# The last stage of a graph kernel, finished in three parts of its nodes, with the output bias on TensorE

## The chip, the cores and the metric

The kernel runs on one NeuronCore of a Trainium2 chip. The metric is the device time of one execution in microseconds; of several executions the median is taken. PE is TensorE, DVE is VectorE, ACT is ScalarE, POOL is GpSimd, SP is SyncE, which only issues DMAs here.

## What is computed

A graph of 6250 nodes with 128 features each and 200000 edges goes through a graph convolution of five rounds, a residual with a row normalisation, an attention over the edges with eight heads, and a second residual with a row normalisation. The change concerns only the end of the attention layer and what follows it:

```python
def _layernorm(x, axis=-1, eps=1e-05):
    m = jnp.mean(x, axis=axis, keepdims=True)
    v = jnp.var(x, axis=axis, keepdims=True)
    return (x - m) / jnp.sqrt(v + eps)
...
        w = es / (denom[row] + 1e-08)
        msg = w[..., None] * V[col]
        out = jax.ops.segment_sum(msg, row, num_segments=n).reshape(n, -1)
        return out @ wo + bo
...
    x = _layernorm(x + _L1_gnn_ref(x, edge_index, edge_attr_64, ...), axis=-1)
    return x
```

## The kernel before

The program is one chain of stages. Every engine runs its part of each stage in program order: adjacency, convolution, `project` (first normalisation, queries, keys and values), `attend` (attention over the edges) and `finish`. Each part is a Python function for one engine (`dve_fin`, `pe_fin`, `act_fin`, `sp_fin`), and the engines are joined by semaphores, so the order on an engine is the order in which the code stands.

Nodes lie in tiles of 128 rows: `NB` = 49 tiles, the last with 106 nodes. `BATCHES` groups them by four: batches 0 to 11 have four tiles, batch 12 has one. `x1` holds the first layer's output (in the profile it is called `deg`, whose memory it uses), `acc` the attention's sums for each node, 128 values and 8 denominators (`h` in the profile).

`finish` works batch by batch, with two PSUM banks for the transposes (`PS[:, n % 2]`) and two for the products (`PS[:, 2 + n % 2]`):

- DVE, `weigh(n)` (L2132): divides a batch's sums by their denominators into `o`, tile by tile.
- PE, in `pe_fin`: transposes the batch (L2105), and then, one batch behind, `products(n - 1)` (L2096) multiplies the previous batch by `wo`. A product in fp32 shows as two matmul records, a transpose as one.
- ACT (L2116): evacuates the transposed batch from PSUM to `ot`.
- DVE, `residual(n)`: adds the product to `x1` (L2140), adds the bias `bo` (L2142), and takes the statistics of each tile (`bn_stats`, L2144).

DVE's order is weigh 0, weigh 1, and for each n: weigh n + 2, residual n. Behind the last batch DVE aggregates the statistics of all 49 tiles (L2154), adds epsilon (L1406), lets ACT take all square roots in one instruction (L2118), takes reciprocals (L1409), and normalises the 49 tiles one by one in place (L2158). SP stores each batch of four tiles when its tiles are normalised (L2086, the last one at L2088), 256 KB each.

`L` (`Chain.link`) makes DVE wait for its own instruction before it goes on. In `project` the first layer is normalised in another way, which the change takes over: `GROUPS` cuts the nodes into three parts, `to_root(g)` aggregates a part's statistics, ACT takes its roots, `scales(g)` makes scale and bias of each node, and ACT normalises tiles with an Identity activation, with the scale and bias as pointers (L1487). `x1_ready` counts the 49 tiles of that stage, `x1_scales_ready` its three parts.

Of the kernel before, what the change touches and what calls it, by code (L numbers as in the profile page):

```python
# [5 lines left out]
FP32 = mybir.dt.float32  # L6
# [4 lines left out]
ALU = mybir.AluOpType  # L11
# [3 lines left out]
P = 128  # L15
# [92 lines left out]
class Kernel:  # L108
# [5 lines left out]
    def sem(self, name):  # L114
        if name not in self.sems:
            self.sems[name] = self.stack.enter_context(self.nc.semaphore(name))
        return self.sems[name]
# [1282 lines left out]
BATCHES = [(t, min(4, NB - t)) for t in range(0, NB, 4)]  # L1400


def normalise(k, v, ch, V, mv, rooted_sem, root_sem, x1):

    L = ch.link
    L(V.tensor_scalar(mv[:, :, 2], mv[:, :, 1], EPS, None, ALU.add))  # L1406
    V.memset(k.vecs[:, 3:4], 0.0).then_inc(root_sem, 1)
    v.wait_ge(rooted_sem, 1)
    L(V.reciprocal(mv[:, :, 2], mv[:, :, 3]))  # L1409


def project(k, stack):

    nc, sem, PS, io = k.nc, k.sem, k.ps, k.io
# [652 lines left out]
def finish(k, out):  # L2067

    nc, sem, PS, io = k.nc, k.sem, k.ps, k.io
    with ExitStack() as s:  # L2070
# [7 lines left out]
        acc = k.h[:, :].rearrange("p (t c) -> p t c", c=MW)  # L2078
        ready, turned, ot_ready, prod, taken = (sem("f_" + n) for n in ("ready", "turned", "ot_ready", "products", "taken"))
        root, rooted, normal, stored = (sem("f_" + n) for n in ("to_root", "rooted", "normal", "stored"))  # L2080
        def sp_fin(sp):
            full = len(BATCHES) - 1
            for n, (t, m) in enumerate(BATCHES):
                sp.wait_ge(normal, t + m)
                if n < full:
                    sp.dma_start(out[t * P:(t + m) * P, :].rearrange("(t p) f -> p t f", p=P), x1[:, t:t + m, :]).then_inc(stored, 16)  # L2086
                else:
                    sp.dma_start(out[t * P:N, :], x1[0:NL, t, :]).then_inc(stored, 16)  # L2088
            sp.wait_ge(stored, 16 * len(BATCHES))

        def products(pe, n):
            pe.wait_ge(ot_ready, n + 1)
            if n >= 2:
                pe.wait_ge(taken, n - 1)
            for x in range(BATCHES[n][1]):
                last = nc.tensor.matmul(PS[:, 2 + n % 2, x * P:(x + 1) * P], ot[:, n % 2, x, :], wo[:, :], start=True, stop=True)  # L2096
            last.then_inc(prod, 1)

        def pe_fin(pe):
# [9 lines left out]
            products(pe, len(BATCHES) - 1)  # L2109

        def act_fin(act):
            for n, (t, m) in enumerate(BATCHES):
                act.wait_ge(turned, n + 1)
                if n >= 2:
                    act.wait_ge(prod, n - 1)
                nc.scalar.activation(ot[:, n % 2, 0:m, :].rearrange("p j c -> p (j c)"), PS[:, n % 2, 0:m * P], ACT.Copy).then_inc(ot_ready, 1)  # L2116
            act.wait_ge(root, 1)
            nc.scalar.activation(mv[:, :, 3], mv[:, :, 2], ACT.Sqrt).then_inc(rooted, 1)  # L2118

        def dve_fin(v):  # L2120
            V = nc.vector
            ch = Chain(v, sem("dve_chain"), k.links)
            L = ch.link
            L(V.tensor_scalar(inv[:, :, :], acc[:, :, D:MW], 1e-8, None, ALU.add))
            L(V.reciprocal(inv[:, :, :].rearrange("p t h -> p (t h)"), inv[:, :, :].rearrange("p t h -> p (t h)")))

            def weigh(n):
                t, m = BATCHES[n]
                if n >= 2:
                    v.wait_ge(turned, n - 1)  # L2130
                for x in range(m):
                    last = V.tensor_tensor(o[:, n % 2, x, :].rearrange("p (h d) -> p h d", d=DK), acc[:, t + x, 0:D].rearrange("p (h d) -> p h d", d=DK),  # L2132
                                           inv[:, t + x, :].rearrange("p (h o) -> p h o", o=1).broadcast_to([P, HEADS, DK]), ALU.mult)
                last.then_inc(ready, 1)

            def residual(n):
                t, m = BATCHES[n]
                rows = x1[:, t:t + m, :]
                v.wait_ge(prod, n + 1)
                V.tensor_tensor(rows, rows, PS[:, 2 + n % 2, 0:m * P].rearrange("p (t f) -> p t f", f=D), ALU.add).then_inc(taken, 1)  # L2140
                v.wait_ge(taken, n + 1)
                L(V.tensor_tensor(rows, rows, bo[:, :].rearrange("p (o f) -> p o f", o=1).broadcast_to([P, m, D]), ALU.add))  # L2142
                for x in range(t, t + m):
                    last = V.bn_stats(st[:, x, :], x1[:, x, :])  # L2144
                return last
            weigh(0)
            weigh(1)
            for n in range(len(BATCHES)):
                if n + 2 < len(BATCHES):
                    weigh(n + 2)  # L2150
                last = residual(n)
            L(V.memset(k.vecs[:, 0:1], 0.0))
            for x in range(NB):
                last = V.bn_aggr(mv[:, x, 0:2], st[:, x, :])  # L2154
            L(last)
            normalise(k, v, ch, V, mv, rooted, root, x1)
            for x in range(NB):
                V.tensor_scalar(x1[:, x, :], x1[:, x, :], mv[:, x, 0:1], mv[:, x, 2:3], ALU.subtract, ALU.mult).then_inc(normal, 1)  # L2158

        return dve_fin, pe_fin, act_fin, sp_fin  # L2160
# [29 lines left out]
```

## Time and profile before

| | us |
|---|---|
| median of 3 runs | 4229.77 |
| the runs | 4227.85 to 4234.28 |
| the profiled execution, its own time | 4231.56 |
| its span in the profile | 4229.8 |
| `finish` within the span, from its first instruction on DVE (4165.31) | 64.5 |

| engine | busy, us | share of the span |
|---|---|---|
| PE | 3654.2 | 86% |
| DVE | 2605.3 | 62% |
| ACT | 1613.4 | 38% |
| POOL | 2980.4 | 70% |

The profile is of one execution. Busy time of PE is modelled from pipelined instructions. The shares are over all stages together; `finish` is the last 1.5% of the span, and nothing follows it.

### The profile page before, as it was taken

Reading aid. Unit: us, or ns where it says so; the run is one execution under the profiler, and the core shown is the slowest. Engines: PE = TensorE matmul, PEld = TensorE weight load, DVE = VectorE, ACT = ScalarE, POOL = GpSimd, SP = SyncE. Lnnn points to the kernel's source line nnn. Section 1 sums busy time; section 2 is a strip of 40 time slices with the busy share of each in tenths; the row PEclk is TensorE's granted clock in tenths of the full one; section 3 lists DMA queues with packets and bytes.
Section 4 is the critical chain, followed back from the end, with each engine's and each line's share of the span. In section 5 each row is a group of like instructions: output and inputs, shape, how many; then the busy total and the mean of one; then the engine's idle time right before and its main releaser. Section 6 shows DMA issues by size and latency. Waiting matters only on the chain.

```text
span 4229.8 us, 87319 instructions
## 1 busy us (share of the span) xinstructions
PE 3654.2 (86%) x23947; PEld 2567.9 (61%) x23948; DVE 2605.3 (62%) x5758; ACT 1613.4 (38%) x4192; POOL 2980.4 (70%) x2979
## 2 busy tenths in 40 slices
PE   5557777259999999999997799999999999999993
PEld 3234444134454544544544488888888888888883
DVE  8999999131131221311313588888888888888887
ACT  0046666130010100100101466666666666666661
POOL 3148788777777777777777477777777777777770
PEclk8979999679999999999998899999999999999997
DMA  9635465469999999899997366666666666666661
GB/s 371 236 106 197 184 223 186 143 227 356 340 312 357 314 333 357 296 358 330 329 357 237 119 177 178 179 178 179 177 177 177 180 179 178 176 179 178 179 179 46
DMA packets 496864, 969.13 MB, mean 229 GB/s; under 512 B 279879, under 2 KB 297235, under 8 KB 494888
## 3 DMA queue, kind: packets, MB, share of 16 engines
q1 hardware_dynamic: 346872, 630.29, 44.8%
q0 software_dynamic: 118768, 243.12, 19.3%
q10 hardware_dynamic: 31168, 95.09, 6.8%
q8 instruction: 20, 0.33, 0.0%
q14 instruction: 36, 0.29, 0.0%
HBM read 767.81 MB, written 200.41 MB: 229 GB/s over the span
## 4 chain that ended last, share of the span: by engine, by line
PE 44%; POOL 31%; issue 13%; DVE 3%; DMA 2%; ACT 1%; DVEq 0%; POOLq 0%; ACTq 0%; SPq 0%
POOL records L1037 26%; PE ps L1158 12%; PE ps L1816 7%; PE ps L1834 7%; PE ps L1820 6%; POOL kv L1755 5%; PE ps L1809 3%; PE ps L1826 2%; PE ps L1789 2%; PE ps L1787 2%; PE ps L1444 1%; DMA records<-recs,pos 1%; PE ps L1136 1%; DMA kv<-kv_table,rec 1%; PE ps L1798 1%
## 5 line engine op out<-in xcount | busy, mean ns | idle before, releaser
L1037 POOL DMA_INDIRECT records<-recs,pos x1562 | 1586.7, 1016 | 480.7 <-issue 470.3
L1755 POOL DMA_INDIRECT kv<-kv_table,rec x1314 | 1311.2, 998 | 481.3 <-issue 440.7
L1158 PE MATMUL ps<-adj,mh 128*128 128x500 f16 (+1 forms) x6370 | 1308.3, 366 | 7.0 <-DVE mh L1309 6.1
L1158 PEld LDWEIGHTS ps<-adj,mh 128*128 128x128 f16 x6370 | 619.4, 97 | 674.8 <-DVE mh L1309 6.3
L1330 DVE TENSOR_TENSOR adj<-adj,quarter 128x128 f16<-128x128 f16 (+25 forms) x305 | 45.8, 209 | 764.7 <-DMA adj<-adj_full 756.8
L1820 PE MATMUL ps<-we,at 128*128 128x256 f32 x1616 | 466.3, 381 | 0.0
L1196 ACT ACTIVATE sc<-sc 128x1 f32<-128x1 f32 x6 | 1.2, 203 | 1216.1 <-DVE sc L1278 973.1
L1834 PE MATMUL ps<-msg,ohf 128*128 128x136 f32 x3232 | 449.0, 282 | 7.8 <-DVE msg L2006 7.8
L1816 PE MATMUL ps<-qn,oht 128*128 x3232 | 446.1, 281 | 4.2 <-ACT at L1883 1.2
L1816 PEld LDWEIGHTS ps<-qn,oht 128*128 128x128 f32 x3232 | 392.7, 192 | 47.4 <-issue 46.7
L1834 PEld LDWEIGHTS ps<-msg,ohf 128*128 128x128 f32 x3232 | 404.9, 191 | 8.9 <-DVE h L2024 8.8
L870 ACT ACTIVATE blk<-ps 128x490 f16<-128x490 f32 x625 | 335.9, 586 | 182.5 <-PE ps L799 180.7
L1998 DVE TENSOR_TENSOR kq<-kv,ps 128x384 f32<-128x384 f32 (+1 forms) x404 | 237.3, 587 | 120.6 <-ACT kq L1896 108.8
L2001 DVE TENSOR_REDUCE scores<-kq 128x32 f32<-128x512 f32 x404 | 277.0, 686 | 22.9
L1999 DVE TENSOR_TENSOR kq<-kq,ps 128x512 f32<-128x512 f32 x404 | 277.4, 687 | 13.9
L2006 DVE TENSOR_TENSOR msg<-kv,msg 128x512 f32<-128x512 f32 x405 | 276.9, 684 | 0.3 <-ACT msg L1925 0.3
L1809 PE MATMUL ps<-x1t,spot_t 128*128 128x128 f32 x1212 | 206.4, 293 | 58.2 <-issue 54.3
L1820 PEld LDWEIGHTS ps<-we,at 128*128 128x128 f32 x1616 | 253.3, 192 | 5.2
L1876 ACT ACTIVATE oht<-ps 128x512 f32<-128x512 bf16 x404 | 237.4, 588 | 0.9 <-PE ps L1789 0.9
L1896 ACT ACTIVATE kq<-ps,x1t 128x128 f32<-128x128 f32 x303 | 111.4, 368 | 327.9 <-PE ps L1820 327.9
L1809 PEld LDWEIGHTS ps<-x1t,spot_t 128*128 128x128 f32 x1212 | 158.4, 190 | 101.4 <-issue 97.2
L1975 DVE TENSOR_TENSOR oh<-iota_b,rec 128x512 bf16<-128x512 bf16 x405 | 170.6, 421 | 76.1 <-issue 70.4
(328 smaller groups left out, 5075.0 us busy)
## 6 DMA issues: line engine op xcount, KB each, us to landing
adj<-adj_full SPq DMA_DIRECT2D x420, 875.0 KB, 6.2
x1t<-kv_table SPq DMA_DIRECT2D x303, 256.0 KB
adj_full<-blk SPq DMA_DIRECT2D x12, 6125.0 KB, 19.0
records<-deg ACTq DMA_DIRECT2D x1, 56576.0 KB, 170.4
rec<-records SPq DMA_DIRECT2D x404, 136.0 KB
records<-recs,pos POOLq DMA_INDIRECT x1562
recs<-in_edge_attr ACTq DMA_DIRECT2D x18, 1344.0 KB, 13.3
kv<-kv_table,rec POOLq DMA_INDIRECT x1314
```

The source lines that it names most:

```text
L870: A.activation(to[:, :, y * WD:(y + 1) * WD], PS[:, slot, 0:WC].rearrange("p (d h) -> p h d", d=WD)[:, 0:NB, :], ACT.Copy, scale=0.25).the ...
L1037: G.indirect_dma_start(out=k.rec_d, out_offset=bass.IndirectOffsetOnAxis(ap=k.pos[:, at:at + 1], axis=0), in_=k.recs[:, q, j, :], in_offse ...
L1158: last = mm(bank, mh[:, part, hi, :], adj[:, c, x * width:(x + 1) * width], start=(hi == 0 and part == 0), stop=True, skip_group_check=True)
L1755: G.indirect_dma_start(out=kv[:, q, j, :], out_offset=None, in_=k.kv_d, in_offset=bass.IndirectOffsetOnAxis(ap=rec[:, q, j, RD:RD + 1].bit ...
L1809: last = mm(PS[:, 6 + q % S, VALUE], spot_t[:, q % S, h, :], window[:, x, h, D:2 * D], start=(h == 0), stop=(h == 1))
L1816: mm(PS[:, 2 + q % S, j * P:(j + 1) * P], oht[:, q % S, j, :], k.qn[:, bass.ds(b[j // 2], 1), :].rearrange("p a c -> p (a c)"), start=True ...
L1820: last = mm(PS[:, 4 + q % S, j * P:(j + 2) * P], at[:, q % S, j // 2, :], we[:, :, :].rearrange("p j d -> p (j d)"), start=True, stop=not ...
L1834: last = mm(PS[:, 6 + q % S, j // 2 * MW:(j // 2 + 1) * MW], ohf[:, q, j, :], msg[:, q, j, :], start=(j % 2 == 0), stop=(j % 2 == 1))
L1876: A.activation(oht[:, q % S, :, :].rearrange("p j c -> p (j c)"), T_OH[q % S], ACT.Copy)
L1999: ch.link(V.tensor_tensor(kq[:, q % S, :, :], kq[:, q % S, :, :], PS[:, 2 + q % S, :].rearrange("p (j c) -> p j c", c=D), ALU.mult))
L2001: V.tensor_reduce(sc[:, q % S, :], kq[:, q % S, :, :].rearrange("p j (h d) -> p (j h) d", d=DK), AX.X, ALU.add).then_inc(S_["scored"], 1)
L2006: return V.tensor_tensor(split(msg[:, q, tiles, 0:D]), split(kv[:, q, tiles, D:2 * D]), msg[:, q, tiles, D:MW].rearrange("p j (h o) -> p j ...
```

## The change

The final normalisation is done in three parts of the nodes: batches 0 to 4 (tiles 0 to 19), 5 to 8 (20 to 35) and 9 to 12 (36 to 48). The bias is added on PE: a matmul of a row of ones by the bias row accumulates onto each tile's product in PSUM, and L2142 is gone. When the last residual of a part is done, DVE aggregates its statistics (`to_root`), and ACT takes its roots at a fixed place between its evacuations. DVE makes the scales of parts 0 and 1 one batch later (`scales`). ACT normalises their tiles in place: batches 0 to 4 between its evacuations 7 to 12, batches 5 to 8 behind them, with the roots of the last part between batch 6 and batch 7. The last part of 13 tiles is normalised by DVE as before. SP stores batches 0 to 6 by ACT's count and then 9, 7, 10, 8, 11, 12 by either engine's. `normalise`, used only here, is removed with two small memsets.

```diff
--- before.py
+++ after.py
@@ -1400,15 +1400,6 @@
 BATCHES = [(t, min(4, NB - t)) for t in range(0, NB, 4)]
 
 
-def normalise(k, v, ch, V, mv, rooted_sem, root_sem, x1):
-
-    L = ch.link
-    L(V.tensor_scalar(mv[:, :, 2], mv[:, :, 1], EPS, None, ALU.add))
-    V.memset(k.vecs[:, 3:4], 0.0).then_inc(root_sem, 1)
-    v.wait_ge(rooted_sem, 1)
-    L(V.reciprocal(mv[:, :, 2], mv[:, :, 3]))
-
-
 def project(k, stack):
 
     nc, sem, PS, io = k.nc, k.sem, k.ps, k.io
@@ -2078,10 +2069,19 @@
         acc = k.h[:, :].rearrange("p (t c) -> p t c", c=MW)
         ready, turned, ot_ready, prod, taken = (sem("f_" + n) for n in ("ready", "turned", "ot_ready", "products", "taken"))
         root, rooted, normal, stored = (sem("f_" + n) for n in ("to_root", "rooted", "normal", "stored"))
+        scaled, x1_ready = sem("x1_scales_ready"), sem("x1_ready")
+        ones = sb("ones_f", [1, P], FP32)
+        parts = (range(0, 5), range(5, 9), range(9, 13))
+        own = BATCHES[parts[2][0]][0]
+        span = lambda part: (BATCHES[part[0]][0], sum(BATCHES[part[-1]]))
         def sp_fin(sp):
             full = len(BATCHES) - 1
-            for n, (t, m) in enumerate(BATCHES):
-                sp.wait_ge(normal, t + m)
+            for n in (0, 1, 2, 3, 4, 5, 6, 9, 7, 10, 8, 11, 12):
+                t, m = BATCHES[n]
+                if n in parts[2]:
+                    sp.wait_ge(normal, t + m - own)
+                else:
+                    sp.wait_ge(x1_ready, NB + t + m)
                 if n < full:
                     sp.dma_start(out[t * P:(t + m) * P, :].rearrange("(t p) f -> p t f", p=P), x1[:, t:t + m, :]).then_inc(stored, 16)
                 else:
@@ -2093,7 +2093,9 @@
             if n >= 2:
                 pe.wait_ge(taken, n - 1)
             for x in range(BATCHES[n][1]):
-                last = nc.tensor.matmul(PS[:, 2 + n % 2, x * P:(x + 1) * P], ot[:, n % 2, x, :], wo[:, :], start=True, stop=True)
+                to = PS[:, 2 + n % 2, x * P:(x + 1) * P]
+                nc.tensor.matmul(to, ot[:, n % 2, x, :], wo[:, :], start=True, stop=False)
+                last = nc.tensor.matmul(to, ones[0:1, :], bo[0:1, :], start=False, stop=True)
             last.then_inc(prod, 1)
 
         def pe_fin(pe):
@@ -2109,18 +2111,46 @@
             products(pe, len(BATCHES) - 1)
 
         def act_fin(act):
-            for n, (t, m) in enumerate(BATCHES):
+            def evacuate(n):
+                m = BATCHES[n][1]
                 act.wait_ge(turned, n + 1)
                 if n >= 2:
                     act.wait_ge(prod, n - 1)
                 nc.scalar.activation(ot[:, n % 2, 0:m, :].rearrange("p j c -> p (j c)"), PS[:, n % 2, 0:m * P], ACT.Copy).then_inc(ot_ready, 1)
-            act.wait_ge(root, 1)
-            nc.scalar.activation(mv[:, :, 3], mv[:, :, 2], ACT.Sqrt).then_inc(rooted, 1)
+
+            def roots(g):
+                a, e = span(parts[g])
+                act.wait_ge(root, g + 1)
+                nc.scalar.activation(mv[:, a:e, 3], mv[:, a:e, 2], ACT.Sqrt).then_inc(rooted, 1)
+
+            def normalised(n):
+                t, m = BATCHES[n]
+                for x in range(t, t + m):
+                    nc.scalar.activation(x1[:, x, :], x1[:, x, :], ACT.Identity, bias=mv[:, x, 3:4], scale=mv[:, x, 2:3]).then_inc(x1_ready, 1)
+            for n in range(7):
+                evacuate(n)
+            roots(0)
+            evacuate(7)
+            act.wait_ge(scaled, len(GROUPS) + 1)
+            for n in range(3):
+                normalised(n)
+                evacuate(8 + n)
+            roots(1)
+            for n in (3, 4):
+                normalised(n)
+                evacuate(8 + n)
+            act.wait_ge(scaled, len(GROUPS) + 2)
+            normalised(5)
+            normalised(6)
+            roots(2)
+            normalised(7)
+            normalised(8)
 
         def dve_fin(v):
             V = nc.vector
             ch = Chain(v, sem("dve_chain"), k.links)
             L = ch.link
+            V.memset(ones[:, :], 1.0)
             L(V.tensor_scalar(inv[:, :, :], acc[:, :, D:MW], 1e-8, None, ALU.add))
             L(V.reciprocal(inv[:, :, :].rearrange("p t h -> p (t h)"), inv[:, :, :].rearrange("p t h -> p (t h)")))
 
@@ -2139,22 +2169,37 @@
                 v.wait_ge(prod, n + 1)
                 V.tensor_tensor(rows, rows, PS[:, 2 + n % 2, 0:m * P].rearrange("p (t f) -> p t f", f=D), ALU.add).then_inc(taken, 1)
                 v.wait_ge(taken, n + 1)
-                L(V.tensor_tensor(rows, rows, bo[:, :].rearrange("p (o f) -> p o f", o=1).broadcast_to([P, m, D]), ALU.add))
                 for x in range(t, t + m):
                     last = V.bn_stats(st[:, x, :], x1[:, x, :])
                 return last
+            def to_root(g, last):
+                a, e = span(parts[g])
+                L(last)
+                for x in range(a, e):
+                    last = V.bn_aggr(mv[:, x, 0:2], st[:, x, :])
+                L(last)
+                V.tensor_scalar(mv[:, a:e, 2], mv[:, a:e, 1], EPS, None, ALU.add).then_inc(root, 1)
+
+            def scales(g):
+                a, e = span(parts[g])
+                v.wait_ge(rooted, g + 1)
+                L(V.reciprocal(mv[:, a:e, 2], mv[:, a:e, 3]))
+                V.scalar_tensor_tensor(mv[:, a:e, 3], mv[:, a:e, 0], -1.0, mv[:, a:e, 2], ALU.mult, ALU.mult).then_inc(scaled, 1)
             weigh(0)
             weigh(1)
             for n in range(len(BATCHES)):
                 if n + 2 < len(BATCHES):
                     weigh(n + 2)
                 last = residual(n)
-            L(V.memset(k.vecs[:, 0:1], 0.0))
-            for x in range(NB):
-                last = V.bn_aggr(mv[:, x, 0:2], st[:, x, :])
-            L(last)
-            normalise(k, v, ch, V, mv, rooted, root, x1)
-            for x in range(NB):
+                for g in (0, 1):
+                    if n == parts[g][-1] + 1:
+                        scales(g)
+                for g in range(len(parts)):
+                    if n == parts[g][-1]:
+                        to_root(g, last)
+            v.wait_ge(rooted, 3)
+            L(V.reciprocal(mv[:, own:NB, 2], mv[:, own:NB, 3]))
+            for x in range(own, NB):
                 V.tensor_scalar(x1[:, x, :], x1[:, x, :], mv[:, x, 0:1], mv[:, x, 2:3], ALU.subtract, ALU.mult).then_inc(normal, 1)
 
         return dve_fin, pe_fin, act_fin, sp_fin
```

## Rows read from the trace of the kernel before

**Rows 1.** The page: busy us of each engine, share of the span, instructions
```profile
PE 3654.2 (86%) x23947; PEld 2567.9 (61%) x23948; DVE 2605.3 (62%) x5758; ACT 1613.4 (38%) x4192; POOL 2980.4 (70%) x2979
```

**Rows 2.** Stretches: length, busy us of PE, PEld, DVE, ACT, POOL; clock, DMA share, GB/s
```profile
4180.00:4200.00 20.00, 10.46 (x83) 9.13 (x81) 19.52 (x67) 4.18 (x7) 0.00 (x0) 1.00 0.00 1
...
4215.00:4230.00 15.00, 0.00 (x0) 0.00 (x0) 10.72 (x42) 0.00 (x0) 0.00 (x0) 0.50 0.79 213
```

**Rows 3.** The chain of waits in `finish`: start, us, what was waited for
```profile
4169.50 1.97 PE ps L2105 x8
...
4174.87 0.87 DVE st_f L2144 x4
4175.74 0.80 DVE o L2132 x4
4176.54 0.61 DVE deg L2140
...
4177.17 0.70 DVE deg L2142
...
4177.90 0.87 DVE st_f L2144 x4
...
4208.51 3.35 DVE mv_f L2154 x49
```

**Rows 4.** Timeline of the last 30 us: start, us, engine, line, operation, idle before
```profile
4213.07 12.65 DVE L2158 TENSOR_SCALAR deg<-deg,mv_f 128x128 f32<-128x128 f32 x49
4214.21 11.65 SPq L2086 DMA_DIRECT2D out<-deg  x12
4225.91 0.45 SPq L2088 DMA_DIRECT2D out<-deg  x1
```

**Rows 5.** Timeline where the first layer is normalised (in `project`), 2322 to 2337 us
```profile
2322.64 0.87 DVE L1516 BATCH_NORM_STATS2 st<-deg 128x6 f32<-128x128 f32 x4
...
2324.83 0.75 DVE L1512 SCALAR_TENSOR_TENSOR deg<-ps,vecs,x_rows 128x512 f32<-128x512 f32 x1
...
2326.40 0.24 DVE L1530 RECIPROCAL mv<-mv 128x16 f32<-128x16 f32 x1
...
2326.78 0.74 DVE L1512 SCALAR_TENSOR_TENSOR deg<-ps,vecs,x_rows 128x512 f32<-128x512 f32 x1
2326.90 6.27 ACT L1487 ACTIVATE deg<-deg,mv 128x128 f32<-128x128 f32 x16 [1.70 <-DVE mv L1531]
```

**Rows 6.** Three lines of matmuls: records, ns (min, median, max), first and last, forms
```profile
L1777 PE MATMUL ps<-x_rows x2: 507/507/507, 2403.6 to 2404.0; 1*128 1x416 f32 x2
...
L1444 PE MATMUL ps<-wqkv,x1t x98: 486/486/1008, 2345.1 to 2401.3; 128*128 128x384 f32 x98
...
L2096 PE MATMUL ps<-wo,ot x98: 274/275/579, 4171.3 to 4204.4; 128*128 128x128 f32 x98
```

**Rows 7.** Timeline of PE and ACT around product 0 and one later batch
```profile
4171.31 2.08 PE L2096 MATMUL ps<-wo,ot 128*128 128x128 f32 x8
...
4179.62 0.66 PE L2105 MATMUL ps<-ident,o 128*128 128x128 f32 x4 [1.48 <-DVE o L2132]
...
4180.11 1.06 PE L2096 MATMUL ps<-wo,ot 128*128 128x128 f32 x8
...
4180.31 0.60 ACT L2116 ACTIVATE ot<-ps 128x512 f32<-128x512 f32 x1 [2.43 <-PE ps L2105]
```

**Rows 8.** The 0.2 us in which the granted clock rose (the number before DMA)
```profile
4173.80:4174.00 0.20, 0.20 (x3) 0.20 (x2) 0.20 (x1) 0.00 (x0) 0.00 (x0) 0.54 0.00 0
```

**Rows 9.** Single microseconds of the stores: the last two columns are DMA share, GB/s
```profile
4219.00:4220.00 1.00, 0.00 (x0) 0.00 (x0) 1.00 (x6) 0.00 (x0) 0.00 (x0) 0.50 0.92 255
...
4227.00:4228.00 1.00, 0.00 (x0) 0.00 (x0) 0.00 (x0) 0.00 (x0) 0.00 (x0) 0.50 0.48 123
```

**Rows 10.** DMA from 4204 to 4230 us, in 40 slices, and by queue
```profile
GB/s 0 0 0 0 0 0 0 0 0 0 0 0 0 0 0 13 0 239 229 285 242 238 291 234 254 269 236 275 251 235 289 236 241 289 235 271 32 35 17 0
...
q1 hardware_dynamic: 6444, 3.20, 45.7%
```

## Prediction

> **What bounds the kernel now.** I read the page first, then the end of the span by stretches, then the chain of waits from 4165 us on, and last the timeline of a single batch. The page says that DVE is busy 62% of 4229.8 us and PE 86% [rows 1], but the diff touches only `finish`, so that average decides nothing. The stretches show where its stage lies: in 4180 to 4200 us DVE works 19.52 of 20 us, PE about half of them, ACT 4.18; from 4215 us on DVE works on and the DMA engines are 0.79 busy [rows 2]. The chain enters the stage at 4165.31 us and stays on DVE but for PE's first transposes (1.97 us, [rows 3]) and first product, one square root on ACT, and the last store. One batch of four tiles costs DVE 3.03 us (4174.87 to 4177.90): four statistics 0.79, weighing 0.79, residual add 0.72, bias add 0.73, each from its start to the next start [rows 3]. After the last batch come 49 aggregations (3.35 us, to 4211.86 [rows 3]), the scale up to 4213.07 (1.21 us), and 49 tiles normalised in 12.65 us, 0.259 us apart. DVE ends at 4225.72 us; the last store is issued at 4225.91 us and the span ends 3.9 us behind that [rows 4]. So the whole stage is some 64.5 us, all of it exposed.
>
> **What the change takes off DVE.** The bias add: 12 full batches at 0.73 us, and the one-tile batch at 0.3: 9.1 us. The statistics then wait for the residual add through the wait that stands there already, which is the 0.72. Normalising parts 0 and 1: 36 of 49 tiles at 0.259 us: 9.3 us. Together 18.4 us.
>
> **What splitting costs DVE.** The aggregations stay 49 in all. The stage that normalises the first layer is written in the same way and shows the price of a cut: from the end of the statistics (2322.64 + 0.87 = 2323.51) to the next add at 2324.83 us are 1.32 us for 16 tiles, of which 16 x 3.35 / 49 = 1.09 are aggregations, so 0.23 us a cut; reciprocal and scale take 2326.40 to 2326.78, 0.38 us [rows 5], and some 0.07 more for 20 tiles. Two cuts and two scales are 1.3 us. The last part gains: 13 tiles need no second multiplication, a root and a reciprocal of 13 columns each about 0.23 us, in place of about 0.3 and 0.5 for 49; with the small memset gone about 0.5 us. Net 0.8 us lost. The memset of the ones row is one more 0.06 us at the start.
>
> **What PE gets.** Each tile's product gets a second matmul, ones (one row) by bias (one row), into the same place. In fp32 each is two matmul records: 98 records for 49 tiles now, 196 afterwards. Does one row instead of 128 make it cheap? The nearest rows are the only one-row matmuls of the trace: 507 ns for 416 columns, against 486 ns for 384 columns with 128 rows [rows 6]. So no: I price a bias record as a product record. Eight of these take 1.06 us with the clock at 2.4 GHz, the last one's 0.27 us among them, 0.112 us apiece; the bias adds 8 x 0.112 = 0.90 us a batch, and the PE work of a batch is 0.49 (transposes to first product) + 1.79 = 2.28 us [rows 7]. The bounds of the unknown are nothing (the one-row records hide between the others) and twice the price (weights alternate between the attention rows and the ones).
>
> *At the start.* The first product runs at a granted clock of 0.50 (1.2 GHz) and the clock rises to 1.00 (2.4 GHz) at about 4174.0 us, after PE had been busy without a gap since 4169.50 [rows 3, 8]. Product 0 starts at 4171.31; at half clock a record is about 0.23 us (8 in 2.08 [rows 7]), so about 12 of 16 fit before the rise and the rest take 0.5 us and the last one's drain: it ends at about 4174.6 instead of 4173.39. That is on the path: 1.2 us.
>
> *In the loop.* Product n stands on PE behind transpose n+1, that waits for weighing n+1, which DVE ends just before residual n-1. From the end of a weighing PE needs 0.14 us to start, and 1.55 us to the end of the next product now (4179.62 to 4181.17 us) [rows 7]; with the bias 2.45. A round from weighing n+1 through product n, residual and statistics n (1.51) to weighing n+3 (0.79) is 0.14 + 2.45 + 0.03 + 1.51 + 0.79 = 4.92 us, and spans two batches: 2.46 us a batch. DVE alone needs 2.30, PE alone 2.28. So the cover of PE's work is gone by 0.16 us a batch where nothing else pauses DVE; where DVE cuts a part it is back. Laid out batch by batch, DVE waits 0.3 us before residuals 2, 4 and 7, and 0.45 to 0.5 before 10 and 11 (no weighing is left there to fill the time): 1.9 us.
>
> **What ACT gets.** A tile with pointer bias and scale: 478 ns, but 16 in a row in 6.27 us, 0.387 us apart [rows 5]. Four of them and one evacuation (0.60 [rows 7]) are 2.2 us against a batch of 2.46, and an evacuation may be late by nearly the time of the next transpose before PE misses it; I lay it out and find product n never waiting for it. The root of a part stands behind evacuations that are due before it. ACT's table load ahead of the root moves from behind the last evacuation to behind number 6, where ACT waits for part 0 anyway. After the last root ACT has 8 tiles (3.2 us), DVE 13 (3.4 us) and a reciprocal: they end together, DVE last.
> The trace has the same tile operation on both engines: 0.259 us on DVE, 0.387 on ACT [rows 4, 5]. The Trainium skill ("ScalarE: Activation LUTs", Rules for kernel authors) speaks against such a move: additions and multiplications belong on VectorE. By that rule the 36 tiles would stay on DVE, and the gain be 9.3 us smaller; by the rows the slower engine has 80% of this stage idle, so the move pays.
>
> **DVE's end.** 18.4 - 0.8 - 0.1 - 1.2 - 1.9 = 14.4 us: 4225.7 - 14.4 = 4211.3 us.
>
> **The stores.** Before, stores leave at the pace of DVE, 256 KB each 1.03 us, and the DMA engines move 255 GB/s at a share of 0.92 [rows 9]: they are nearly full. Over the stage 3.20 MB took 45.7% of 26 us, which makes 269 GB/s when busy [rows 9, 10]. Now seven batches leave early and in the open. But store 9 comes with the fourth DVE tile, at 4209.0 us, and five full stores and the 53 KB rest (1.365 MB) are due by 4211.5. Data begin 0.75 us behind the issue (4214.21 to about 4215 [rows 4, 10]); 1.365 MB at 269 GB/s are 5.1 us (at 255, 5.35): 4214.8 us. Before, a full rate would have ended at 4227.5 us and the span at 4229.8: 2.3 us more [rows 9]. That makes 4217.1 us, against 4211.3 + 4.1 = 4215.4 if DVE set it. Of 14.4 us, 12.7 remain. SP's order puts store 9 before 7 and 10 before 8; a store that is ready waits at most 0.3 us behind another's wait, while the queue is full anyway.
>
> **The time.** The profiled execution took 4231.56 us, span 4229.8; the median of the runs is 4229.77, 1.8 us less. Span 4229.8 - 12.7 = 4217.1; on the median 4217.1, which I round to 4217. A difference under 0.2% (8.5 us) can't be told from none here.
>
> **Rivals.** *Stores drain freely* (0.20): the engines take more than 269 GB/s once several stores are queued. For it: single slices of the stage show up to 291 [rows 10]; against it: a share of 0.92 at 255. DVE then sets the end: 4215.4. The Trainium skill ("DMA: Bandwidth & Descriptors", Specifications) gives 435 GB/s as the ceiling of the fabric; an estimate by it has the 1.365 MB gone in 3.1 us, which is this case; no row of the stage shows such a rate.
> *The bias matmuls hide* (0.12): the loop runs at DVE's 2.30 and the start costs little: 1.9 + 1.2 us less, 4214.
> *They cost twice* (0.12): 1.8 us a batch on PE, which then bounds with 0.49 + 0.90 + 1.80 = 3.2 us a batch; eleven batches later product 11 is 5.5 us late: 4222.6, within 0.2% of no change. For it: no row alternates weights of one row and of 128.
> *The clock stays down* (0.03), the other side: pauses at the cuts keep PE at 1.2 GHz. A batch is then 0.9 + 16 x 0.23 = 4.6 us of PE; from product 0 at 4175.6 eleven more end at 4226, 22 us later than forecast: 4239, slower by 0.2%. It decides from the clock of the stretch on; PE would pass DVE's 2.30 by far. Against it: the clock is 1.00 through 4180 to 4200 us with PE busy half of the time [rows 2], and the change makes it busier.
> The forecast itself has 0.50; 0.03 is left for an evacuation that comes late or an end on ACT, a few us at most.
>
> **Range and chances.** Both gains together (-1.7 - 3.1) give 4212.3, the dear matmul 4222.6; runs of the kernel before scatter by some us. 4211.5 to 4222.5. Faster by over 0.2% is below 4221.3: 0.85; same 0.12; slower 0.03.
>
> **What the profile of after would show.** The residual's period on DVE near 2.46 us, pairs of batches 4.9; a PE row of bias records at the mean of the product's; product 0 ending at 4174.6; the clock 1.00 from 4174; ACT tiles 0.387 apart; DVE's last instruction at 4211.3; the last store landing over 4.5 us behind its issue with the DMA share above 0.9 from 4210 to 4215. A PE that is idle between batches, a last store that lands in 3.9 us, or a half clock would each name the rival that holds.

## The result, and the profile after

The changed kernel takes 4260.53 us (median of 6 runs, 4255.67 to 4262.9) against 4229.32 for the kernel before: a ratio of 1.0073 (95% interval 1.006 to 1.0086). It is 31 us slower; forecast were 12 us less. The profiled execution took 4255.67 us, its span 4253.6.

The attention ahead of `finish` varies by some us from one execution to the next, and the stage starts at another time in each profile. So in what follows a kernel's stage is measured from the start of its first `inv` instruction on DVE to the end of the span: 64.5 us before (4165.31 to 4229.8), 96.0 us after (4157.64 to 4253.6). The difference of 31.5 us is the whole loss.

The page after, cut to the span, the engines and the granted clock in 40 slices:

```profile
span 4253.6 us, 87509 instructions
...
PE 3715.6 (87%) x24045; PEld 2607.6 (61%) x24046; DVE 2588.5 (61%) x5714; ACT 1626.6 (38%) x4230; POOL 2971.8 (70%) x2979
...
PEclk8979999689999999999998899999999999999995
```

PE has 61 us more busy time than before [rows 1], for 98 records more, and the granted clock of the last slice is a 5 (0.5); in the kernel before it was a 7. Stretches of the stage (us, then busy time of PE, PEld, DVE, ACT, POOL, the granted clock, DMA share, GB/s), to hold against [rows 2]:

```profile
core 0: us, PE busy (x) PEld busy (x) DVE busy (x) ACT busy (x) POOL busy (x), PEclk, DMA share, GB/s
4160.00:4180.00 20.00, 18.25 (x58) 13.44 (x58) 8.08 (x31) 2.39 (x4) 0.00 (x0) 0.50 0.00 1
4180.00:4200.00 20.00, 20.00 (x63) 14.39 (x62) 8.69 (x48) 3.31 (x5) 0.00 (x0) 0.50 0.00 0
```

Before, DVE was full and PE half busy at a clock of 1.00. Now PE is busy for 20.00 of 20 us at a clock of 0.50, and DVE for 8.69. The chain of waits of the changed kernel (start, us, what was waited for; L2107 are the transposes, L2097 the products, L2098 the bias matmuls):

```profile
4161.76 1.97 PE ps L2107 x8
4163.73 0.63 PE ps L2097 x2
...
4169.41 1.04 PE ps L2107 x4
4170.46 0.43 PE ps L2097 x2
4170.89 0.72 PE ps L2098 x2
...
4240.68 0.70 DVE deg L2170
...
4245.43 2.56 DVE deg L2203 x10
```

From 4161.76 to 4240.68 us it never leaves PE. A batch is four transposes and eight pairs of records and takes 6.53 us (4169.41 to 4175.95 us, when the next transposes start), where it was 3.03 us on DVE [rows 3]. A pair that follows one of the other kind takes 0.72 us. The timeline shows what is between them:

```profile
4164.28 0.50 PEld L2098 LDWEIGHTS ps<-bo,ones_f 1*128 1x128 f32 x2 [0.22 <-issue]
4164.28 0.79 PE L2098 MATMUL ps<-bo,ones_f 1*128 1x128 f32 x2
4165.00 0.50 PEld L2097 LDWEIGHTS ps<-wo,ot 128*128 128x128 f32 x2 [0.22 <-issue]
4165.01 0.80 PE L2097 MATMUL ps<-wo,ot 128*128 128x128 f32 x2
...
4169.45 0.69 DVE L2170 TENSOR_TENSOR deg<-deg,ps 128x512 f32<-128x512 f32 x1 [5.64 <-PE ps L2098]
```

The weight loads of each pair begin 0.22 us after PEld fell idle, with "issue" as the reason. PE's busy time hides this wait: a pair's records last 0.79 us in the profile, and the next pair begins after 0.72 us. In [rows 7] eight records of products follow each other without such a wait, 2.08 us at the clock of 0.50 with the first one's start and the last one's drain; in e2 below, pairs start 0.43 us apart at the same clock. So a pair pays about 0.29 us extra whenever it follows one of the other kind. A batch has eight such changes: seven between products and bias matmuls, and one from the last bias matmul to the transposes, which have 128 rows as the products have.

The end of the stage is as the prediction had it. Timeline, and one microsecond of the DMA engines:

```profile
4244.17 3.17 ACT L2129 ACTIVATE deg<-deg,mv_f 128x128 f32<-128x128 f32 x8
...
4244.57 3.42 DVE L2203 TENSOR_SCALAR deg<-deg,mv_f 128x128 f32<-128x128 f32 x13
...
4248.98 0.84 SPq L2088 DMA_DIRECT2D out<-deg  x1
```

```profile
4249.00:4250.00 1.00, 0.00 (x0) 0.00 (x0) 0.00 (x0) 0.00 (x0) 0.00 (x0) 0.50 1.07 287
```

ACT's eight tiles and DVE's thirteen end within 0.7 us of each other, and the stores that come with them keep the DMA engines busy, at 287 GB/s and a share of 1.07.

### The profile page after: what moved, and what is told of

Its sections match the earlier page's. It is cut to its first block, busy times and chain, and to the rows that moved or that the text cites. A ratio compares the mean times of both kernels' runs of the same rounds, so it can differ in the third digit from the quotient of the medians.

```text
span 4253.6 us, 87509 instructions
## 1 busy us (share of the span) xinstructions
PE 3715.6 (87%) x24045; PEld 2607.6 (61%) x24046; DVE 2588.5 (61%) x5714; ACT 1626.6 (38%) x4230; POOL 2971.8 (70%) x2979
## 3 DMA queue, kind: packets, MB, share of 16 engines
q1 hardware_dynamic: 346872, 630.29, 44.8%
## 4 chain that ended last, share of the span: by engine, by line
POOL 38%; PE 35%; issue 16%; DVE 2%; DMA 2%; ACT 1%; DVEq 0%; POOLq 0%; ACTq 0%; SPq 0%
POOL records L1037 31%; POOL kv L1746 7%; PE ps L1807 6%; PE ps L1158 6%; PE ps L1825 6%; PE ps L1811 5%; PE ps L1800 3%; PE ps L1817 2%; PE ps L1780 1%; PE ps L1778 1%; PE ps L2098 1%; PE ps L1435 1%; PE ps L2097 1%; DMA kv<-kv_table,rec 1%; DMA records<-recs,pos 1%
```

## The experiments

Each median of e1 to e12 stands against the kernel before on the same chip (4230.3 to 4230.8 us). The stage is read from one profile of each kernel. An interval that holds 1 (e3, e7) shows no difference from the kernel before.

| kernel | bias on | stage, us | median, us | ratio (95% interval) |
|---|---|---|---|---|
| before | DVE | 64.5 | 4229.3 to 4230.8 | |
| changed | PE, one row | 96.0 | 4260.5 | 1.0073 (1.006 to 1.0086) |
| e1, parts only | DVE | 58.0 | 4226.3 | 0.9987 (0.9978 to 0.9997) |
| e2, full rows | PE, 128 rows | 52.1 | 4219.1 | 0.9972 (0.9959 to 0.9984) |
| e3, grouped | PE, one row, four first | 64.7 | 4232.2 | 1.0004 (0.9995 to 1.0014) |
| e4, bias only, no parts | PE, one row | 106.4 | 4273.4 | 1.0098 (1.0081 to 1.0115) |
| e5, 32 rows | PE, 32 rows | 96.0 | 4259.4 | 1.0073 (1.0056 to 1.0089) |
| e6, 64 rows | PE, 64 rows | 95.9 | 4262.1 | 1.0075 (1.0059 to 1.0092) |
| e7, one matmul a batch | PE, one row | 67.0 | 4230.8 | 1.0001 (0.9991 to 1.001) |
| e8, one matmul a batch | PE, 128 rows | 52.1 | 4216.5 | 0.9967 (0.9955 to 0.998) |
| e9, warm, one row | PE, one row | 92.8 | 4260.1 | 1.0072 (1.0055 to 1.0089) |
| e10, warm, full rows | PE, 128 rows | 50.3 | 4216.5 | 0.9968 (0.9955 to 0.998) |
| e11, fewer stores | PE, 128 rows | 50.3 | 4217.1 | 0.9967 (0.9954 to 0.9979) |
| e12, bias early | DVE, in the projection | 49.7 | 4216.3 | 0.9966 (0.9954 to 0.9979) |

### Parts or bias: e1 and e4

e1 keeps the parts and gives the bias back to DVE:

```diff
-                to = PS[:, 2 + n % 2, x * P:(x + 1) * P]
-                nc.tensor.matmul(to, ot[:, n % 2, x, :], wo[:, :], start=True, stop=False)
-                last = nc.tensor.matmul(to, ones[0:1, :], bo[0:1, :], start=False, stop=True)
+                last = nc.tensor.matmul(to, ot[:, n % 2, x, :], wo[:, :], start=True, stop=True)
...
+                L(V.tensor_tensor(rows, rows, bo[:, :].rearrange("p (o f) -> p o f", o=1).broadcast_to([P, m, D]), ALU.add))
```

> The three parts are kept, the bias goes back to DVE (an add of 128x512 for each batch) and PE has the products alone. Theory: the loss comes from PE alone, and the parts do what the prediction says. Then the clock rises to 1.00 as before, a batch costs DVE 3.03 us, and the sum is 9.3 (36 tiles moved) - 0.8 (cuts) = 8.5 us at the end of DVE, of which some 1.7 go back to queued stores: 4229.3 - 6.8 = 4222.5 us. Rival: the parts themselves cost (ACT's tiles between its evacuations hold up PE, or the cuts hold up DVE): then this kernel stays above 4229.

The stage took 58.0 us, 6.5 less than before (6.8 expected); the ratio of 0.9987 is 5.5 us (its interval 1.3 to 9.3), the medians lie 4.1 us apart. So the parts gain, and the stage puts their size near the price. e4 is the other half, the kernel before with L2142 removed and the two matmuls of the change in its `products`:

> The kernel before with the one-row bias matmuls alone: no parts, DVE normalises all 49 tiles. Theory: PE sets the pace with 6.53 us a batch just as in the changed kernel, and the end costs 10.5 us more than there (36 aggregations more, 36 tiles more at 0.259 us less what stood in the cuts): about 4271 us. Rival: PE's slow pace comes from ACT and PE meeting in the parts; then this kernel runs at 3 us a batch and stays near 4229.

4273 us; its residuals are 6.53 us apart, with no part, no cut and no tile of ACT in the kernel (timeline of DVE):

```profile
4178.29 0.69 DVE L2144 TENSOR_TENSOR deg<-deg,ps 128x512 f32<-128x512 f32 x1 [5.65 <-PE ps L2099]
...
4184.82 0.69 DVE L2144 TENSOR_TENSOR deg<-deg,ps 128x512 f32<-128x512 f32 x1 [4.14 <-PE ps L2099]
```

So the loss is in the bias matmuls alone.

### Rows or target: e2

e2 gives the bias matmul 128 rows: the identity by the bias, which lies in every partition.

```diff
-                last = nc.tensor.matmul(to, ones[0:1, :], bo[0:1, :], start=False, stop=True)
+                last = nc.tensor.matmul(to, k.ident[:, :], bo[:, :], start=False, stop=True)
...
-            V.memset(ones[:, :], 1.0)
```

> The bias matmul has 128 rows instead of one: the identity as weights and the bias, which lies in all partitions, as the moving operand. As many matmuls, in the same order, onto the same targets. Theory 1 (rows): PE's array runs empty whenever a matmul of one row count follows one of another (128 and 1), and the one-row matmuls keep the granted clock down. Then the pair of records falls from 0.72 us to 0.23 at the clock of 1.00, a batch from 6.53 us to about 2.46, and the time is that of the prediction, 4217 us. Rival, theory 2 (target): the second matmul waits for the first because it accumulates onto the place that the first has just written. Then a pair of records still takes about 0.72 us at half clock and the time stays near 4260.

4219.1 us. As many matmuls in the same order onto the same places, with 128 rows and the identity in place of the ones: its timeline (L2097 product, L2098 bias, L2169 residual) and one stretch:

```profile
4173.42 0.64 PE L2097 MATMUL ps<-wo,ot 128*128 128x128 f32 x2
4173.84 0.63 PE L2098 MATMUL ps<-bo,ident 128*128 128x128 f32 x2
...
4175.84 0.69 DVE L2169 TENSOR_TENSOR deg<-deg,ps 128x512 f32<-128x512 f32 x1 [3.18 <-PE ps L2098]
...
4176.30 0.39 PE L2098 MATMUL ps<-bo,ident 128*128 128x128 f32 x2
...
4176.52 0.39 PE L2097 MATMUL ps<-wo,ot 128*128 128x128 f32 x2
...
4180.77 0.69 DVE L2169 TENSOR_TENSOR deg<-deg,ps 128x512 f32<-128x512 f32 x1 [0.24 <-PE ps L2098]
...
4185.69 0.69 DVE L2169 TENSOR_TENSOR deg<-deg,ps 128x512 f32<-128x512 f32 x1 [0.23 <-PE ps L2098]
```

```profile
4180.00:4200.00 20.00, 17.41 (x147) 16.31 (x145) 18.92 (x101) 10.31 (x21) 0.00 (x0) 1.00 0.15 41
```

At a clock of 0.50 a pair follows the other kind after 0.43 us (4173.42 to 4173.84 us), at 1.00 after 0.22 us; the clock rises to 1.00 at about 4175.3 us, and two batches take 4.93 us. Theory 2 has fallen: accumulating onto the place that was just written costs nothing that shows. Of the changed kernel's 96.0 us of the stage, 43.9 go when the bias matmul is given 128 rows. The edit changes its values as well as its rows, and 128 rows of ones of 1/128 weren't run. Against the values as the cause: transposes by the identity and products by `wo` follow each other without the wait in the changed kernel too, and e5 and e6 below have other values than one in more rows and wait just as long.

### How much is the change of rows, how much the clock: e3 and e7

e3 puts the four one-row matmuls of a batch first, and the products accumulate onto them:

```diff
...
+            for x in range(m):
+                nc.tensor.matmul(PS[:, 2 + n % 2, x * P:(x + 1) * P], ones[0:1, :], bo[0:1, :], start=x == 0, stop=False)
+            for x in range(m):
+                last = nc.tensor.matmul(PS[:, 2 + n % 2, x * P:(x + 1) * P], ot[:, n % 2, x, :], wo[:, :], start=False, stop=x == m - 1)
```

> As many one-row matmuls as in the changed kernel, but the four of a batch come first and then its four products: two changes of the row count a batch instead of eight. Theory 1: six changes less at about 0.27 us each (0.72 us a pair against 0.45 without a change) are 1.6 us a batch, 6.53 to 4.9 us if the clock stays at 0.50, which makes 4240 us; if the clock rises once the gaps are gone, the batch comes to about 2.8 us and the time to 4220. Theory 2 (target): no matmul follows another onto the same place any more, so all of the loss in pace goes: 4.6 us a batch at half clock, 4236 us. Whether the clock rises tells if the one-row matmuls or the gaps hold it down.

4232.2 us, between the two times named (4240 and 4220), because the clock did both. Timeline of PE (L2108 transposes, L2097 bias, L2099 products) and three stretches:

```profile
4175.19 1.06 PE L2108 MATMUL ps<-ident,o 128*128 128x128 f32 x4
4176.18 2.07 PE L2097 MATMUL ps<-bo,ones_f 1*128 1x128 f32 x8
...
4180.05 1.06 PE L2108 MATMUL ps<-ident,o 128*128 128x128 f32 x4
...
4183.11 0.60 PE L2108 MATMUL ps<-ident,o 128*128 128x128 f32 x4
4183.65 1.15 PE L2097 MATMUL ps<-bo,ones_f 1*128 1x128 f32 x8
...
4185.77 0.66 PE L2108 MATMUL ps<-ident,o 128*128 128x128 f32 x4
```

```profile
4178.00:4180.00 2.00, 2.00 (x10) 1.82 (x9) 0.00 (x0) 0.00 (x0) 0.00 (x0) 0.50 0.00 0
...
4182.00:4184.00 2.00, 2.00 (x17) 1.71 (x16) 1.37 (x5) 0.25 (x1) 0.00 (x0) 1.00 0.03 8
...
4196.00:4198.00 2.00, 2.00 (x10) 1.67 (x10) 1.62 (x6) 1.11 (x3) 0.00 (x0) 0.50 0.36 104
```

At 0.50 a batch takes 4.86 us (4175.19 to 4180.05) and at 1.00 2.66 us (4183.11 to 4185.77). The first number against 6.53 is the price of six changes of the row count fewer: 1.67 us, 0.28 each, which agrees with the 0.29 read from the pairs. The second step, 2.2 us a batch, is the clock. In the changed kernel both come together: 6.53 us against e2's 2.46, 4.07 us a batch; over eleven batches that is 44.8 us, near the 43.9 by which the stages differ.

e7 makes one one-row matmul of 512 columns of the four:

```diff
...
+            nc.tensor.matmul(PS[:, 2 + n % 2, 0:m * P].rearrange("p (t f) -> p t f", f=D), ones[0:1, :], bo[0:1, :].rearrange("p (o f) -> p o f", o=1).broadcast_to([1, m, D]), start=True, stop=False)
+            for x in range(m):
+                last = nc.tensor.matmul(PS[:, 2 + n % 2, x * P:(x + 1) * P], ot[:, n % 2, x, :], wo[:, :], start=False, stop=x == m - 1)
```

> One one-row matmul of 512 columns for the whole batch, ahead of its four products: two records instead of eight for the bias, two changes of rows a batch, as many one-row columns as in the changed kernel. Work of PE in a batch: 0.49 + 0.43 + 0.90 + two changes of 0.17 = 2.0 us at clock 1.00, less than DVE's 2.30; at clock 0.50 0.96 + 0.86 + 1.81 + 0.54 = 4.2 us. Theory B (columns with one row count little for the clock, whatever their records): the clock goes up and down as in the grouped run, and the time lies between, about 4224 us. Rival (it is the number of one-row matmuls or of changes that holds the clock down): clock 1.00 throughout and 4217 us.

4230.8 us, like e3, later than the expected 4224 and unlike the rival. Its batches too are 4.86 us at 0.50 and 2.6 at 1.00, and its clock goes up and down. The 0.43 us for the bias in the expectation was wrong: 512 columns are two records of 0.43 us at the clock of 1.00, so 0.86, hardly less than the 0.90 of eight records of 128 columns. Fewer records bought nothing here; the time went with the columns.

### How many rows: e5 and e6

The bias matmul with 32 and with 64 rows (`ones[0:32, :]` holding 1/32, `bo[0:32, :]`; the same with 64):

> The changed kernel with 32 rows in the bias matmul: ones of 1/32 in 32 partitions by the bias in 32 partitions. The full-row run has settled that a change of the row count costs and the target doesn't; here the size is asked. Theory A (any change of rows costs the same, and fewer rows than 128 keep the clock down): 0.72 us a pair of records and 4260 us as with one row. Theory B (the cost or the clock goes with the number of rows that work): the clock rises at some time in the stage, to 0.45 us a pair with the change (0.22 of work, 0.18 of change, as in the grouped run at clock 1.00), a batch of about 4 us, and the time lies near 4233 us.

> The same with 64 rows (ones of 1/64). Theory A: 4260 us, as with one row. Theory B: the clock is up from near the start on, the pair still costs the change: 0.40 us, a batch of 0.5 + 8 x 0.40 = 3.7 us, 4230 us. If the pair is 0.22 us at clock 1.00, half of the rows is no change of rows to PE, and the time is that of the full rows, 4219.

Theory A in both: 4259.4 and 4262.1 us. Timeline of PE and one stretch of the kernel with 64 rows:

```profile
4180.81 0.80 PE L2097 MATMUL ps<-wo,ot 128*128 128x128 f32 x2
4181.53 0.79 PE L2098 MATMUL ps<-bo,ones_f 64*128 64x128 f32 x2
```

```profile
4180.00:4200.00 20.00, 20.00 (x62) 14.54 (x62) 7.06 (x27) 1.79 (x3) 0.00 (x0) 0.50 0.00 1
```

0.72 us a pair and a clock of 0.50, no better than with one row. Half of the rows isn't half of the loss: somewhere above 64 rows the loss goes, and what was tried doesn't say where.

### Does a raised clock last: e9 and e10

Ten matmuls with 128 rows onto PSUM bank 5, which nobody reads, at the head of `pe_fin`; e9 is the changed kernel with them, e10 the full-row kernel with them:

```diff
         def pe_fin(pe):
+            for _ in range(10):
+                nc.tensor.matmul(PS[:, 5, 0:P], k.ident[:, :], wo[:, :], start=True, stop=True)
```

> The changed kernel, one-row bias matmuls and all, with ten full-row matmuls on PE ahead of the stage, onto a PSUM bank that nobody reads, in the time in which PE waits for the reciprocal. They should bring the granted clock to 1.00 before the first transpose. Question: does the pattern of one-row and full-row matmuls only fail to raise the clock, or does it bring a raised clock down? If it holds 1.00, a pair of records takes about 0.40 us, a batch 3.7, and the time is about 4228 us. If the clock falls back to 0.50, as it did in the grouped run, the batch is 6.53 us again and the time 4257 us. I expect the fall.

4260.1 us. PE's timeline (L2103 are the added matmuls) and three microseconds of the clock:

```profile
4160.97 3.94 PE L2103 MATMUL ps<-wo,ident 128*128 128x128 f32 x20
...
4167.42 0.49 PE L2097 MATMUL ps<-wo,ot 128*128 128x128 f32 x2
4167.84 0.48 PE L2098 MATMUL ps<-bo,ones_f 1*128 1x128 f32 x2
...
4173.45 0.79 PE L2098 MATMUL ps<-bo,ones_f 1*128 1x128 f32 x2
4174.17 0.80 PE L2097 MATMUL ps<-wo,ot 128*128 128x128 f32 x2
```

```profile
4170.00:4171.00 1.00, 1.00 (x6) 0.76 (x7) 0.14 (x1) 0.00 (x0) 0.00 (x0) 1.00 0.00 0
4171.00:4172.00 1.00, 1.00 (x6) 0.78 (x4) 0.96 (x4) 0.32 (x1) 0.00 (x0) 0.51 0.00 0
4172.00:4173.00 1.00, 1.00 (x4) 0.77 (x4) 1.00 (x7) 0.28 (x1) 0.00 (x0) 0.50 0.00 0
```

The clock was at 1.00 when the first product came, and a pair then took 0.42 us, against 0.22 for full rows: the change of rows costs 0.2 us at this clock too. At about 4171.0 us, some 3.5 us into this pattern and without a gap in PE's busy time since it began, the clock fell to 0.50, and at the end of the stage it was still there. So the pattern doesn't only fail to raise the clock, it doesn't hold a raised one either. PE had also waited 1.17 us ahead of the first transpose (to 4166.08 us); such a wait alone is not enough, for in e2 PE waited 1.86 us at the first cut (to 4189.83) and the clock stayed at 1.00.

> The full-row bias with the same ten matmuls ahead. The clock should be at 1.00 from the first transpose on, which takes what is left of the late start: transposes 1.97 to about 1.2 us, product 0 from 3.4 (16 records, mostly at 1.2 GHz) to 2.0 us. The first residual comes 2.1 us earlier, and the time is 4217 us against 4219. Rival: the wait ahead of the stage is too short or ends too late for them, and they hold up the first transpose: then it is no faster than the full-row run.

4216.5 us, as expected; the first residual comes 7.70 us into the stage (4162.37 to 4170.07), 9.42 in e2: 1.7 us of the 2.1 expected. The last added matmul ends about 0.6 us before the first transpose.

### The stores at the end: e11

e2 without the stores of batches 7 and 8, so that its output lacks eight tiles:

> The full-row bias, but the stores of batches 7 and 8 are left out (their 8 tiles of the output are not written; they are computed). It sizes the queue of stores at the end: 0.84 MB instead of 1.365 MB come with DVE's last tiles. If the DMA engines set the end, at 287 GB/s, the span ends 1.5 to 1.8 us earlier with DVE's end where it was: 4.1 us from DVE's last instruction to the end of the span instead of 5.6. Rival: the 5.6 us are the latency of the last store and its issue on SP: then nothing moves.

```profile
4207.97 3.42 DVE L2203 TENSOR_SCALAR deg<-deg,mv_f 128x128 f32<-128x128 f32 x13
4211.57 0.45 SPq L2088 DMA_DIRECT2D out<-deg  x1
```

From DVE's last instruction (4211.39) to the end of the span (4215.5) are 4.1 us, as in the kernel before; in e2, e1 and the changed kernel they are 5.6. The queue of stores costs 1.5 us, and the rival, the latency of the last store, has fallen.

### Two other ways to add the bias: e8 and e12

e8 is the full-row bias in one matmul of 512 columns a batch, ahead of the products:

> The same with 128 rows: identity by the bias spread over the batch, one matmul of 512 columns ahead of the four products. This removes what the full-row run still shows: the round of PE and DVE of 4.93 us for two batches (it becomes 4.45, under DVE's 4.60), and half of the late start. Against the full-row run: 1.5 us in the loop and 0.6 at the start: 4217 us. Rival: the stores at the end take all of it, since DVE's last tiles only queue for the DMA engines: then it stays at 4219.

The stage took 52.1 us, no less than e2's, and two batches 4.89 us: the expectation rested on the same wrong 0.43 us as e7's. That the time of 4216.5 us came out near the 4217 expected is luck: the intervals of e8 and e2 overlap, and in the profiles the stage begins at 4163.2 us in e8 and at 4166.4 in e2, by what lies ahead of it.

e12 has no bias matmul at all and takes the bias out of the stage. In the projection DVE adds it to x1, after a batch is transposed:

```diff
                 bias(x)
+                n = x - 9 if x < 18 else {19: 9, 21: 10, 23: 11, 24: 12}.get(x)
+                if n is not None:
+                    t, m = BATCHES[n]
+                    V.tensor_tensor(x1[:, t:t + m, :], x1[:, t:t + m, :], k.bo[:, :].rearrange("p (o f) -> p o f", o=1).broadcast_to([P, m, D]),
+                                    ALU.add).then_inc(sem("output_biased"), 1)
...
```

> The parts of the change without any bias matmul and without the bias add in the stage: DVE adds the bias to the rows of x1 in the projection stage, batch by batch once they are transposed, where DVE waits for PE (2347 to 2402 us). The stage then keeps all of 18.4 us less on DVE, none of the late start, and none of the round of 2.46 us: a batch is 2.30 us, DVE's part of the stage 60.4 - 18.4 + 0.8 = 42.8 us, the stage to the end of the span 48.4 us against 64.5, and the time 4214 us. Rival: the 8.5 us of adds aren't hidden in the projection, where PE and DVE take turns: then up to 4222.

4216.3 us, ratio 0.9966, 14 us less than before and the shortest stage of all, 49.7 us. Its median can't be told from those of e8 and e10. Four rows of its timeline (L2173 residual) and two stretches:

```profile
4171.31 0.69 DVE L2173 TENSOR_TENSOR deg<-deg,ps 128x512 f32<-128x512 f32 x1 [1.87 <-PE ps L2101]
...
4173.62 0.68 DVE L2173 TENSOR_TENSOR deg<-deg,ps 128x512 f32<-128x512 f32 x1
...
4190.22 0.69 DVE L2173 TENSOR_TENSOR deg<-deg,ps 128x512 f32<-128x512 f32 x1 [0.62 <-PE ps L2101]
...
4203.83 3.42 DVE L2206 TENSOR_SCALAR deg<-deg,mv_f 128x128 f32<-128x128 f32 x13
```

```profile
4180.00:4182.00 2.00, 1.34 (x12) 1.34 (x12) 1.97 (x8) 0.63 (x2) 0.00 (x0) 1.00 0.02 4
...
4186.00:4188.00 2.00, 1.34 (x7) 1.05 (x6) 1.93 (x9) 1.47 (x4) 0.00 (x0) 0.50 0.00 0
```

The residuals start 8.1 us into the stage, as before, and are 2.30 us apart. Of the 1.2 us that DVE's part of the stage took beyond the expected 42.8 (it took 44.0), half lies behind the first cut: PE has nothing to do for 2.4 us there, the clock falls to 0.50, and DVE waits 0.62 us for the product ahead of 4190.22. The 8.5 us of adds went into waits of the projection: from its first matmul with `wqkv` to the attention's first one-hot on DVE are 60.9 us in e12 (2345.20 to 2406.11), 61.8 in the kernel before, and 59.2 to 61.9 in the profiles of the others.

## Why the prediction was wrong

**What held.** The parts were priced about right: the expected 8.5 us on DVE and 6.8 at the end of the span were 8.0 and 6.5 in e1. With a bias matmul that costs what the prediction took for it (e2), the rest of its sum stands as well. First residual late by 1.2 us: 1.3. A round of 4.92 us for two batches: 4.93. ACT's tiles 0.387 us apart: eight in 3.18 us. DVE's end 14.4 us earlier: 13.9. From DVE's end to the end of the span 5.8 us: 5.6, with the queue draining at 287 GB/s instead of 269; the rival of stores that drain freely has fallen in e11. In all 12.7 us were expected of the stage and 12.4 came. Moving the tiles to the engine that is slower at them paid, as the rows said. The 435 GB/s of the Trainium skill ("DMA: Bandwidth & Descriptors", Specifications) were reached by no store of this stage: the highest single microsecond shows 295 GB/s (e12). The Trainium skill's rule that the prediction set against the move ("ScalarE: Activation LUTs", Rules for kernel authors) would have cost time here, where VectorE sets the pace: e1's stage is 6.5 us shorter for going against it.

**The step that failed** is one sentence: "So no: I price a bias record as a product record." By it the bias was 0.90 us a batch and PE's work 2.28 us, at a clock of 1.00; PE's batch measured 6.53 us. The price rested on [rows 6], the trace's one-row matmuls (two of its four records are shown there). Those rows were read rightly, and e9's records show it (a one-row pair lasts 0.48 us, a product pair 0.49); but four one-row records that follow each other, in a stretch where PE was otherwise idle, say nothing of a one-row record between two full ones. The price isn't of the record but of the change, and of the clock that goes with it: 0.29 us a change at 0.50, and 0.43 instead of 0.22 us for a pair. The row that was needed, of matmuls with unlike rows side by side at full load, isn't in the trace of before, and the prediction said as much in its rival ("no row alternates weights of one row and of 128"). It still gave that rival only 0.12 and bounded it at twice the price, a number with no row behind it: at 1.00 a bias pair with its two changes is 0.22 + 2 x 0.2, nearly three times the 0.22.

**The second error** was to take the rivals one by one. "They cost twice" was priced at the clock of 1.00 (4222.6 us), "the clock stays down" without a dearer record (4239 us). What happened is both, and they are one cause: 6.53 us a batch against the 3.2 and the 4.6 of the two. Added up they would have made a high end of some 4260 us (4239, and in each of eleven batches eight records of 0.23 us more). That step had failed too: the argument against the half clock, that the change "makes it busier", read the clock off PE's busy time. [rows 2] showed a clock of 1.00 with PE half busy; the changed kernel shows 0.50 with PE fully busy. Nor was it the pauses that the rival named: in the changed kernel PE doesn't pause. They do act where PE has less to do. In e1 and in e12 PE waits 3.16 and 2.43 us at the first cut, and the clock falls to 0.50 behind it (at about 4190.1 and 4185.5 us); in e1 no later residual waits for PE, and in e12 one does, for 0.62 us.

**What stays open.** That one cause moves both is shown for the pattern as a whole, not inside it: whether the clock is held down by the fewer rows or by the 0.2 us between the kinds. e3 and e7 have few changes and many one-row columns, and their clock was up for some 18 us of the stage and down for the rest, with the same batch repeated. What made it change in e3, at 4181.0, 4194.7, 4211.7 and 4215.2 us, isn't known: the first fall comes 2 us behind the pause at the first cut, the second with PE busy throughout. Why the loads wait isn't known. Whether 96 rows would do, and 128 rows of ones instead of the identity, wasn't tried.

## What to carry to other kernels

A matmul that is small in rows isn't small in time, and beside full ones it can be dearer than a full one, as here: if a bias must go through TensorE, try it with all 128 rows (the identity by a bias that lies in every partition, e2), or add it earlier, where an engine waits anyway (e12). When an operation of the change appears in the trace only by itself, its row prices it by itself; the neighbours that it will have need a row of their own, or a bound that holds a change of the clock as well. And rivals that could have one cause belong in one number.

## What the runs showed of the hardware

- A pair of fp32 matmul records with 128 rows that follows a pair with 1, 32 or 64 rows, or the other way round, starts 0.28 to 0.29 us late at a granted clock of 0.50 (0.72 against 0.43 us, the changed kernel, e5, e6 and e2), and with 1 row about 0.2 us late at 1.00 (0.42 us in e9 against 0.22 in e2). The pairs of 128 rows are the measure.
- In that pattern the clock stayed at 0.50 for 80 us with PE busy without a gap, and where it had been raised it fell from 1.00 some 3.5 us after the pattern began (e9). With 128 rows in both it rose 4.7 us after PE's first transpose (e2, 4170.6 to 4175.3 us) and stayed through the loop, over waits of PE of up to 1.9 us. With one-row matmuls in groups it rose and fell again (e3, e7).
- After pauses of PE of 2.4 us (e12, PE busy 5.75 of the 8 us before) and 3.2 us (e1) at the first cut the clock fell as well, 0.9 and 1.3 us after PE had started again.
- Stores of 256 KB with several queued moved 287 GB/s at a DMA share of 1.01 to 1.07 (e2, the changed kernel); one every 1.03 us, 255 GB/s at 0.92 [rows 9].
- Matmuls that accumulate onto the place written just before follow at 0.22 us a pair at a clock of 1.00, as products onto fresh places do (e2; [rows 7]).
